# Three narrow attentions: four score products on four row tiles at once, and VectorE's output step behind both waves

## The reference

```python
q = split_heads(queries @ Wq + bq)
k = split_heads(keys @ Wk + bk)
v = split_heads(values @ Wv + bv)
scores = jnp.einsum('bhqd,bhkd->bhqk', q, k) / jnp.sqrt(jnp.float32(HD))
scores = jnp.where(mask, jnp.float32(-1000000000000000.0), scores)
attn = jax.nn.softmax(scores, axis=-1)
ctx = jnp.einsum('bhqk,bhkd->bhqd', attn, v)
ctx = ctx.transpose(0, 2, 1, 3).reshape(b, sq, d)
return ctx @ Wo + bo
```

## Time and profile before

| | |
|---|---|
| time, median of 3 runs | 1122.97 us (1120.03 to 1124.45) |
| the profiled execution | 1125.25 us, its span 1123.3 us |
| TensorE (PE) busy | 960.0 us, 85% |
| VectorE (DVE) busy | 783.4 us, 70% |
| ScalarE (ACT) busy | 627.3 us, 56% |
| GpSimd (POOL) busy | 197.8 us, 18% |
| chain that ended last, by engine | PE 72%, DVE 17%, ACT 8% |
| score products, line 470 | 192 matmuls, 57.7 us busy |
| row maxima, line 597 | 48, 58.4 us busy, 12.7 us idle before |
| subtraction, line 601 | 48, 58.8 us busy, 7.1 us idle before |

### The profile page before, as it was taken

The page is one execution under the profiler, slowest core; times in us unless marked ns, Lnnn a source line. Parts: engine busy times, 40 slices in busy tenths (PEclk is TensorE's granted clock), DMA queues, the critical chain, the costliest instruction groups (busy, mean ns, idle before and its releaser), DMA issues.

```text
span 1123.3 us, 15610 instructions
## 1 busy us (share of the span) xinstructions
PE 960.0 (85%) x5200; PEld 611.2 (54%) x5200; DVE 783.4 (70%) x1171; ACT 627.3 (56%) x1053; POOL 197.8 (18%) x150
## 2 busy tenths in 40 slices
PE   7989859997897536598898399999778999999998
PEld 3666526664354212265355277777245777777774
DVE  3466447777595767577487667776548888888886
ACT  6356425555455515255565255555457777777776
POOL 0011031321000000000100522421310333333330
PEclk9899979999999758679899699999888999999999
DMA  7000000110000000000000101101100111111100
GB/s 302 1 1 0 1 28 15 42 49 1 1 2 1 0 1 0 0 1 2 0 2 2 49 1 49 48 1 38 37 0 1 37 38 40 53 37 37 37 19 19
DMA packets 9706, 27.95 MB, mean 25 GB/s; under 512 B 1344, under 2 KB 2624, under 8 KB 9536
## 3 DMA queue, kind: packets, MB, share of 16 engines
q1 hardware_dynamic: 9664, 27.37, 7.0%
HBM read 26.84 MB, written 0.52 MB: 24 GB/s over the span
## 4 chain that ended last, share of the span: by engine, by line
PE 72%; DVE 17%; ACT 8%; issue 2%; DMA 0%; POOL 0%; DVEq 0%; ACTq 0%; SPq 0%
PE ps L624 13%; PE ps L626 12%; PE ps L625 12%; PE ps L478 4%; PE ps L470 4%; PE ps L1230 3%; PE ps L184 2%; PE ps L495 2%; PE ps L489 2%; ACT rstd L215 2%; ACT rstd L218 2%; PE ps L193 1%; ACT arena L1300 1%; PE ps L1043 1%; PE ps L994 1%
## 5 line engine op out<-in xcount | busy, mean ns | idle before, releaser
L624 PE MATMUL ps<-parts 128*128 128x512 f32 (+2 forms) x608 | 282.6, 465 | 9.5 <-DVE parts L840 6.4
L626 PE MATMUL ps<-parts 128*128 128x512 f32 (+2 forms) x608 | 242.1, 398 | 0.0
L625 PE MATMUL ps<-parts 128*128 128x512 f32 (+2 forms) x608 | 239.9, 395 | 0.0
L654 ACT ACTIVATE parts<-ps 128x512 fp32r<-128x512 f32 (+1 forms) x256 | 153.1, 598 | 152.9 <-PE ps L626 77.3
L658 DVE TENSOR_TENSOR parts<-ps,parts 128x512 fp32r<-128x512 f32 (+1 forms) x256 | 176.2, 688 | 3.0
L624 PEld LDWEIGHTS ps<-parts 128*128 128x128 f32 (+2 forms) x608 | 116.1, 191 | 47.5 <-DVE parts L658 16.2
L1802 DVE TENSOR_TENSOR ps<-arena,ps 128x512 f32<-128x512 f32 x160 | 111.3, 696 | 33.3 <-DVE parts L658 32.8
L642 POOL TENSOR_TENSOR parts<-ring,zeros 128x1024 fp32r<-128x1024 f32 (+4 forms) x52 | 72.4, 1405 | 345.7 <-PE ps L626 312.9
L626 PEld LDWEIGHTS ps<-parts 128*128 128x128 f32 (+2 forms) x608 | 113.7, 187 | 28.9
L625 PEld LDWEIGHTS ps<-parts 128*128 128x128 f32 (+2 forms) x608 | 114.7, 189 | 23.4
L845 DVE TENSOR_TENSOR ps<-arena,ps 112x512 f32<-112x512 f32 (+1 forms) x96 | 66.8, 696 | 56.4 <-PE ps L626 56.4
(11 more groups left out here) (325 smaller groups left out, 1291.5 us busy)
## 6 DMA issues: line engine op xcount, KB each, us to landing
ring<-m_in SPq DMA_DIRECT2D x20, 512.0 KB, 3.5
ring<-m_up_in SPq DMA_DIRECT2D x8, 448.0 KB, 3.6
pack<-pack_in SPq DMA_DIRECT2D x1, 2058.5 KB, 9.7
ring<-m_up_in SPq DMA_DIRECT2D x8, 256.0 KB, 2.6
ring<-m_down_in SPq DMA_DIRECT2D x8, 224.0 KB, 3.6
ring<-m_down_in SPq DMA_DIRECT2D x8, 128.0 KB, 2.5
pack<-pack_in SPq DMA_DIRECT2D x1, 968.0 KB, 14.0
pack<-pack_in SPq DMA_DIRECT2D x1, 836.0 KB, 11.2
```

Source lines behind the costliest of these rows:

```text
L624: nc.tensor.matmul(dst, w_high, x_high, start=start, stop=False, skip_group_check=True)
L625: nc.tensor.matmul(dst, w_high, x_low, start=False, stop=False, skip_group_check=True)
L626: return nc.tensor.matmul(dst, w_low, x_high, start=False, stop=stop, skip_group_check=True)
L654: nc.scalar.activation(m_hh[0:rows, p], ps[0:rows, src, :], ACT.Copy).then_inc(R(t, "_hh"), 1)
```

## The change

In `narrow_tensor`, `scores` is split: `masks(b, v)` writes the mask rows of one wave, and `scores(b)` issues all four 32-row products of a sequence in one go and signals twice, after the second and the fourth. The order of a sequence in TensorE's queue becomes: turn of wave 0, masks of wave 0 of the next sequence, `weigh`, wait until both waves are subtracted, masks of wave 1, the four products, `total`, turn of wave 1. In `narrow_vector`, `outputs(b - 2)` and the `four_bits` step go behind both waves. `narrow_scalar` stays as it is.

```diff
-            def scores(b, v):
-
-                for r in range(2 * v, 2 * v + 2):
-                    if mask is not None:
-                        rows = mask[:, :] if mask is caus else mask[:, b * P:(b + 1) * P]
+            def masks(b, v):
+
+                if mask is not None:
+                    rows = mask[:, :] if mask is caus else mask[:, b * P:(b + 1) * P]
+                    for r in range(2 * v, 2 * v + 2):
                         mm(bank(r), identb[:, :], rows.unsqueeze(1).to_broadcast([P, GH, P]), start=True, stop=False, skip_group_check=True)
-                for r in range(2 * v, 2 * v + 2):
+
+            def scores(b):
+
+                for r in range(ROWG):
                     at = slice(32 * r, 32 * r + 32)
                     ins = mm(bank(r), a_q[at, b * P:(b + 1) * P], a_kb[at, :, b * P:(b + 1) * P],
                              start=mask is None, stop=True, skip_group_check=True, tile_position=(32 * r, 0))
-                ins.then_inc(R(t, "_scores"), 1)
+                    if r % 2:
+                        ins.then_inc(R(t, "_scores"), 1)
...
+            wait("_q_ready", 1 if rope else 2)
             for v in range(2):
-                wait("_q_ready", 1 if rope else v + 1)
-                scores(0, v)
+                masks(0, v)
+            scores(0)
             for b in range(B):
-                for v in range(2):
-                    w = 2 * b + v
-                    if b + 1 < B:
-                        if b + 1 == HB and v == 0:
-                            wait("_kb1", GH)
-                            wait("_q_ready", 2)
-                        wait("_z", w + 1)
-                        scores(b + 1, v)
-                    if b == 1 and v == 0:
-                        wait("_v_ready", 1)
-                        pe.wait_ge(S("filled"), 8)
-                    if b > 0:
-                        (total if v else weigh)(b - 1)
-                    turn(v, w)
+                turn(0, 2 * b)
+                if b == 1:
+                    wait("_v_ready", 1)
+                    pe.wait_ge(S("filled"), 8)
+                if b + 1 < B:
+                    masks(b + 1, 0)
+                if b > 0:
+                    weigh(b - 1)
+                if b + 1 < B:
+                    if b + 1 == HB:
+                        wait("_kb1", GH)
+                        wait("_q_ready", 2)
+                    wait("_z", 2 * b + 2)
+                    masks(b + 1, 1)
+                    scores(b + 1)
+                if b > 0:
+                    total(b - 1)
+                turn(1, 2 * b + 1)
...
             for b in range(B):
                 for v in range(2):
-                    if v == 1:
-                        if b >= 2:
-                            outputs(b - 2)
-                        if meanwhile:
-                            meanwhile(b)
                     maxima(v, 2 * b + v)
+                if b >= 2:
+                    outputs(b - 2)
+                if meanwhile:
+                    meanwhile(b)
```

## The result

The changed kernel takes 1183.96 us (median of 4 runs, 1181.1 to 1185.67) against 1123.71 for the kernel before (4 runs, 1120.03 to 1126.56): a ratio of 1.0523, 95% interval 1.0496 to 1.055. It is slower by 60 us. The forecast was 1186.

The account below looks back on a forecast made before the run. The prediction took TensorE's full queue to bound the kernel before, and a waiting loop through three engines the changed one. It added 24 us at full clock and 39 for half clock: +63, 1186 us, range 1144 to 1215.

Parts of the forecast that it names:

- What bounds the kernel before: In the narrow attentions x1, x2 and f2, TensorE has no gap; a sequence takes 7.06 us with masks, 6.31 without.
- Four row tiles take what two do: On TensorE, a sequence's four products together take 1.06 us in the queue and 1.13 to the last result.
- estimate of 1.38: Time in us of four row tiles by the skill's factor; the 24 sequences would be some 8 us dearer.
- The loop: Maxima, subtraction, exponential, copy, turn, weigh, scores, next maxima: 7.81 us for x2, 8.79 for x1 and f2.
- Outputs and four_bits cost nothing: On VectorE, outputs (1.20 us) and x1's four_bits steps fit in its wait after 4.86 us, adding nothing.
- The clock: TensorE's idle piece of 2.7 us per sequence makes the clock fall to half repeatedly; +39 us forecast.
- The share: Part of the three attentions at half clock: half of 77 us taken, +39; range a quarter to 85%, chance 0.60.
- 201.9: Sum in us of the three attentions at full clock (69.5, 62.9, 69.5), 22.9 more than the 179.0 before.
- later starts: First maxima of each of the three attentions start about 0.5 us later, 1.5 in all.
- Full clock: Rival: the clock stays full in the attentions despite idle pieces; 1147 us (1143 to 1165), chance 0.18.
- The third rival: The turn doesn't delay TensorE; VectorE's waves and scores set periods of 6.64 and 6.11 us: 1111 us, chance 0.04.

Follow-up runs that it names:

- e5: The kernel before with VectorE's part of the change alone (outputs and four_bits steps behind both waves), TensorE's queue as it was: 1118.10 us, ratio 0.9936.
- e8: e7 with the scores of each attention's first sequences (0 and 1) issued in pairs, each behind its own wave: 1112.00 us, ratio 0.9873.
- e4: The changed kernel with five unused float32 products filling TensorE's idle piece behind the turn of wave 1 in sequences 1 to 6: 1159.08 us, ratio 1.0316.
- e1: The changed kernel with the four score products moved ahead of the turn of wave 0 and weigh, still waiting for both subtractions: 1127.14 us, ratio 1.0022.
- e3: The changed kernel with ScalarE's copy of wave 1 ahead of the exponential of the next sequence's wave 0: 1164.22 us, ratio 1.0365.
- e7: e1 with total moved behind the turn of wave 1: 1121.22 us, ratio 0.9972.
- e2: The changed kernel with outputs and four_bits steps put back between the two waves on VectorE: 1181.21 us, ratio 1.0516.
- e9: e8 with the scores of sequence 2 in pairs too: 1116.24 us, ratio 0.9894.
- e10: e7 with the four products issued as two pairs at the same place, each behind its own masks and wait: 1132.07 us, ratio 1.0051.
- e6: The changed kernel with the products split into two pairs, wave 0's right behind its turn and masks, ahead of weigh: 1158.59 us, ratio 1.0300.

## Why the prediction was right, point by point

- **What bounds the kernel before.** TensorE's queue, in steps of 7.06 and 6.31. e5 leaves these steps as they are although it reorders VectorE; e8 shortens them with less TensorE work. Right for f2 (7.05) and x2 (6.31). For x1 it was an oversight: I doubled half a period, but x1's later steps are 8.55, 8.03, 7.27, 7.74 and 6.47, and TensorE waits there for VectorE's subtraction, 0.65 us ahead of 320.28 and 0.52 ahead of 335.29, with the `four_bits` steps in VectorE's queue. The forecast doesn't rest on it, since it took x1's measured length of 62.15 and put the new loop in its place.
- **Four row tiles take what two do.** 1.14 us against 1.13. Right. The estimate of 1.38 from the Trainium skill's factor of 3.07 ("TensorE: Matmul & The Clock Gate", section "Measured speedup vs the span model") isn't met by these float32 products of 32 x 512: here four tiles cost 0.01 us more than two. What one tile alone takes, no run shows, so the factor itself isn't tested.
- **The loop.** 7.81 and 8.79 worked out (the terms of the second add up to 8.78); 7.80 read in the changed kernel, 7.81 and 8.78 in e4. e1 took ScalarE's operations, the turn and weigh out of the loop, and the step of f2 fell to 7.00; e3 took the copy out, and the step of x2 fell to 7.26. Right, and shown. e7 took `total` out of e1's loop, which is another, and the step fell to 6.64.
- **Outputs and four_bits cost nothing.** e2: right in the changed kernel. In the kernel before, e5 shows that their place is worth some 7 us.
- **The clock.** The mechanism was right: each sequence has one idle piece, of 2.6 to 2.8 us (3.7 in the first, and in x1 and f2 in the second too), and TensorE is at half clock behind 21 of the 24. The share was guessed at a half of the price of 77 us. What was measured is less: the attentions take 236.1 us, which is 34 above the 201.9 that were worked out for full clock, or 44% of 77. The later steps say much the same: a masked step is 10.38, which is 1.6 of the 3.6 above 8.79 (44%); the six later steps of x2 average 8.9, which is 1.1 of 2.7 (about 40%). By attention: 83.5 predicted and 82.0 measured for x1, 73.7 and 70.5 for x2, 83.5 and 83.5 for f2. This is the one term whose size was a choice, and that 1186 came so near to 1184 is partly luck: had the share been a quarter or three quarters, the forecast would have been 19 us off its place with the same mechanism. Nor do the parts meet as well as the sum. The attentions were forecast to grow by 62 us and grew by 57; the 1.5 us of later starts don't show, for the rest of the span shrank by 1.2; and the profiled executions are 56 us apart, the medians 60.
- **The rivals.** Full clock would have been 1147: e4, which fills the idle time but not in the first sequences, gives 1159. The third rival, VectorE's waves with the scores behind them, is no property of the row tiles but of the order, and e7 and e8 reach its steps (6.64). Its price of 1111 was met only by e8, and only after two things that its sum had left out were taken away: the subtraction's wait for the turn, and the late start.

The Trainium skill's warning ("TensorEngine Tiling (Array Packing)", section "PSUM Bottleneck") that emptying PSUM may become the bound is borne out in part in e8: of its step of 6.64 VectorE waits 0.58 us only, and VectorE's two waves with the scores behind them are the loop. In the changed kernel it was a wait and not the work of emptying.

Still open: where e5's gain outside x1 comes from, and what decides how long the clock stays at half in x2, which stood at 17.1 us of half clock in the kernel before, e5, e9 and e10 and at 13.7 in e8, and why three of the eight idle pieces of x2 in the changed kernel had none behind them.

## What to carry to other kernels

When work is merged so that it needs more inputs at once, see what stands ahead of it in its queue: here the four products were free, but behind a turn that waits for a copy that waits for an exponential, they closed a loop through three engines. Write down each loop with every wait in it, the buffers' own included; the longest loop, not the busiest engine, gave the period to within 0.1 us in the changed kernel, e4, e6 and e7, where all waits were in the sum; in e10 it was 0.1 and 0.3 us off. A long idle piece on TensorE cost twice here, by itself and by the slower clock behind it, so a chain that is 0.55 us shorter gave back 20 us in 24 sequences.

## What the runs showed of the hardware

Four row tiles ran at the price of two (1.14 and 1.13 us for 32 x 512 float32 products). In the changed kernel an idle piece of 2.6 to 2.7 us was followed by 3.4 us at a granted clock of 0.50 in each later sequence of x1 and f2, and in x2 in some and not in others. Idle pieces of 1.2 us in e6 had no half clock behind them once its first sequences were over. 2.3 us of needless products in the idle piece took the half clock away in e4: 180 matmuls more (5380 instead of 5200), 25 us less.
